# A four-layer sequence model on one core: the first layer's gated experts computed by picked slots in 39 blocks, gate products in column groups, a capacity search in 14 steps

## The reference, cut to what matters

```python
def _L0_ffn_ref(x, gate_w, w_up, w_down, sg_gate, sg_up, sg_down):
    E, TOP_K, HALF = 8, 2, 192
    logits = xf @ gate_w.T
    topk_logits, topk_idx = jax.lax.top_k(logits, TOP_K)
    topk_w = jax.nn.softmax(topk_logits)
    comb = jnp.zeros((N, E)).at[jnp.arange(N)[:, None], topk_idx].add(topk_w)
    for e in range(E):
        y = jax.nn.silu(xf @ wg[e].T) * (xf @ wu[e].T) @ w_down[e].T
        out = out + comb[:, e:e + 1] * y
    shared = jax.nn.silu(xf @ sg_gate.T) * (xf @ sg_up.T) @ sg_down.T
    return shared + out
```

## Time and profile before

| | us |
|---|---|
| median of 3 runs (lowest to highest) | 3692.75 (3686.59 to 3693.5) |
| the profiled execution, its own time | 3684.66 |
| the span of its records | 3683.3 |
| layer 0 routing, 881.03 to 911.05 of the span | 30.0 |
| layer 0 experts, 911.05 to 1267.51 | 356.5 |
| layer 1 search, 2160.94 to 2238.64 | 77.7 |
| layer 1 slots scattered to first block, 2256.28 to 2302.18 | 45.9 |
| layer 1 experts, 2302.18 to 2414.43 | 112.3 |

### The profile page before, as it was taken

One profiled execution on the slowest core, in us unless ns is written; L12 is line 12 of the kernel. 1 busy time (PEld: TensorE's weight loads), 2 busy tenths in 40 slices (PEclk: granted clock), 3 DMA queues, 4 the chain that ended last, 5 costly groups with the idle time before them and its releaser, 6 DMA issues. The chain is left out here.

```text
span 3683.3 us, 43526 instructions
## 1 busy us (share of the span) xinstructions
PE 2919.2 (79%) x12846; PEld 1023.0 (28%) x12846; DVE 2553.5 (69%) x2911; ACT 1819.9 (49%) x3121; POOL 746.6 (20%) x835
## 2 busy tenths in 40 slices
PE   6499999965999948999999551967877787996766
PEld 3122222213333321222222130822322333332222
DVE  4699999934444459989998153267999984446548
ACT  2288888861222226888888310535555541224233
POOL 3311111100000031111110003604777750000000
PEclk8599999986999968999999755987999997998868
DMA  4210110111000040010000220221000000001010
GB/s 121 80 27 24 27 26 23 27 28 62 0 0 0 0 158 22 24 27 23 25 24 18 57 77 30 59 76 37 6 12 6 12 1 0 0 0 56 0 46 23
DMA packets 112034, 116.61 MB, mean 32 GB/s; under 512 B 37102, under 2 KB 88174, under 8 KB 111516
## 3 DMA queue, kind: packets, MB, share of 16 engines
q1 hardware_dynamic: 97116, 83.65, 7.7%
q0 software_dynamic: 14784, 31.43, 2.9%
HBM read 64.25 MB, written 50.75 MB: 31 GB/s over the span
## 5 line engine op out<-in xcount | busy, mean ns | idle before, releaser
L640 DVE TENSOR_REDUCE a_att_mx<-a_att_s 128x2 f32<-128x1024 f32 x1024 | 1204.9, 1218 | 104.4 <-PE a_att_s L551 91.9
L625 ACT ACTIVATE a_att_pt<-a_att_st 128x512 f32<-128x512 f32 x2048 | 1064.6, 604 | 267.8 <-PE a_att_st L577 246.8
L577 PE MATMUL a_att_st<-a_att_qst,a_att_kst 50*128 50x512 bf16 x2048 | 628.8, 389 | 77.8 <-ACT a_att_pt L625 65.0
L551 PE MATMUL a_att_s<-a_att_kst,a_att_qst 50*128 50x512 bf16 x2048 | 532.1, 402 | 84.1 <-DMA a_att_kst<-a_kstk 51.2
L564 PE MATMUL a_att_av<-a_att_pt,a_att_vst 128*32 128x512 f32 x4096 | 554.1, 614 | 0.0
L577 PEld LDWEIGHTS a_att_st<-a_att_qst,a_att_kst 50*128 50x128 bf16 x2048 | 158.9, 94 | 752.2 <-ACT a_att_pt L625 693.7
L929 DVE TENSOR_TENSOR f_h<-f_sg,f_up 128x512 f32<-128x512 f32 x184 | 126.5, 687 | 309.2 <-ACT f_sg L917 309.2
L917 ACT ACTIVATE f_sg<-f_gp 128x512 f32<-128x512 f32 x184 | 109.9, 597 | 460.9 <-PE f_cp L906 460.9
L1701 POOL TENSOR_TENSOR g_xn<-m2s_hs,m2s_cb 128x1024 f32<-128x1024 f32 x128 | 300.9, 2356 | 119.3 <-DVE m2s_hs L1668 66.9
L1668 DVE TENSOR_TENSOR_SCAN m2s_hs<-m2s_da,m2s_bps 128x1024 f32<-128x1024 f32 x128 | 292.7, 2287 | 4.4
L1584 PE MATMUL m2s_yps<-g_xn,g_ident 128*128 128x512 f32 x512 | 242.7, 596 | 0.9
(11 more groups left out here) (396 smaller groups left out, 3502.5 us busy)
## 6 DMA issues: line engine op xcount, KB each, us to landing
a_att_qst<-a_qstk POOLq DMA_DIRECT2D x128, 100.0 KB, 2.5
a_att_kst<-a_kstk POOLq DMA_DIRECT2D x128, 100.0 KB, 2.5
a_qstk<-a_qkv_part SPq DMA_DIRECT2D x96, 128.0 KB, 1.9
a_kstk<-a_qkv_part SPq DMA_DIRECT2D x96, 128.0 KB, 2.0
a_num<-a_att_oev SPq DMA_DIRECT2D x256, 16.0 KB
a_out_nm<-a_num SPq DMA_DIRECT2D x16, 256.0 KB, 3.3
a_out_rb<-a_rden SPq DMA_DIRECT2D x16, 256.0 KB, 4.4
area<-in_f_w_dram SPq DMA_DIRECT2D x2, 2048.0 KB, 10.2
```

The source lines that it names most:

```text
L551: mm = pe.matmul(s1[:, cut % 2, h, :], qst[u][64 * h:64 * h + STACK, qt * P:(qt + 1) * P], kst[u][64 * h:64 * h + STACK, kh * CH:(kh + 1) ...
L577: pe.matmul(st[:, e % 3, :], kst[u][64 * h:64 * h + STACK, kt * P:(kt + 1) * P], qst[u][64 * h:64 * h + STACK, half * CH:(half + 1) * CH], ...
L625: act.activation(pt[:, e % 16, :], st[:, e % 3, :], ACT.Exp, scale=scale).then_inc(exp_done, 1)
L640: dve.tensor_reduce(mx[:, par, 2 * cut:2 * cut + 2], s1[:, cut % 2, :, :], AX.X, ALU.max).then_inc(s1_used, 1)
```

## The change

1. **Layer 0 by slots.** `top2_stage` and `glu_stage` of layer 0 give way to `pick_stage` and `pick_glu_stage`. Each token is written twice, once for each pick, into slots of the pick's expert: 8192 picks in at most 39 blocks of 256 slots, all of which are computed. The shared expert is computed for all tokens on PE while POOL scatters. Each result row is multiplied by its pick's weight and scattered back; at the end PE adds a token's two rows while it turns them (two accumulated products with the identity) and DVE adds them to `g.xT`.
2. **Gate products in column groups** (class `Logits`, layers 0, 1, 2). The gate, padded to 32 columns by POOL, is now the stationary operand and the tokens move: four chunks go to four groups of 32 output rows of the array. ACT copies the rows, PE transposes them (8 of 128 x 128), and DVE picks out the logits.
3. **Capacity search in 14 steps.** Each step tries three thresholds at once (a quarter, a half and three quarters of the interval) and so settles two bits.
4. `gate0` gets one more 64 KB load; the weights of layer 0 are laid out per expert by 13 loads in place of 4, in the same norm stage.

```diff
+class Logits:
+    def pad(self, pool):
+        pool.memset(self.gate32[:, :], 0.0).then_inc(self.padded, 1)
+        pool.wait_ge(self.padded, 1)
+        pool.tensor_copy(self.gate32[:, 0:self.e], self.gate).then_inc(self.padded, 1)
+    def multiply(self, pe, g):
+        pe.wait_ge(self.padded, 2)
+        for m in range(2):
+            for q in range(4):
+                mm = pe.matmul(self.row_ps[32 * q:32 * q + 32, m, :], self.gate32[:, :], g.xn[:, c * CH:(c + 1) * CH], ...)
+            mm.then_inc(self.rows_ready, 1)
...
+def pick_stage(nc, g, name, w, picked):
+                sp.wait_ge(zeroed, 1)
+                sp.dma_start(sent, zero[:, :].unsqueeze(1).to_broadcast([P, n_rows, PICK_WIDE])).then_inc(cleared, 16)
+                sp.wait_ge(cleared, 16)
+                sp.wait_ge(numbered, 1)
+                sp.dma_start(sent[:, :, P:PICK_WIDE], tail[:, :, :]).then_inc(cleared, 16)
+                sp.wait_ge(cleared, 32)
...
+def pick_glu_stage(nc, g, name, w, picked, ahead):
+            def _(pool):
+                for t in range(2 * NT):
+                    pool.indirect_dma_start(picked.sent, ..., rows[:, t, :], None).then_inc(scattered, 16)
+                for i in range(PICK_BLOCKS):
+                    pool.wait_ge(tails_taken, 2 * (i // 3 + 1))
+                    pool.wait_ge(r_copied, wide * (i + 1))
+                    for j in range(wide):
+                        pool.indirect_dma_start(picked.back, ..., yr[:, i % 3, j, :], None).then_inc(r_sent[i % 3], 16)
+            def _(sp):
+                sp.wait_ge(scattered, 16 * 2 * NT)
+                for k in range(groups):
...
+                    sp.dma_start(xs[:, k % 4, :, :], sent[:, 3 * wide * k:3 * wide * (k + 1), :]).then_inc(x_here[k % 4], 16)
...
+                for c in range(NCH // 2):
+                    for r in range(2):
+                        sp.dma_start(got[:, r, 8 * c:8 * c + 8, :], back[:, r, 8 * c:8 * c + 8, :]).then_inc(got_here[c], 16)
+            def _(act):
+                def take_weights(i):
+                    first = act.value_load(expert_i[0:1, i:i + 1], min_val=0, max_val=7) * per_expert
+                    if i >= ring:
+                        act.wait_ge(y_ready, i - ring + 1)
+                    act.copy(wb[:, i % ring, :], own[:, bass.ds(first, per_expert)]).then_inc(w_copied, 1)
...
+                def take_rows(i):
+                    dve.wait_ge(r_turned, i + 1)
+                    dve.wait_ge(tails_taken, 2 * (i // 3 + 1))
+                    if i >= 3:
+                        dve.wait_ge(r_sent[i % 3], 16 * wide * (i // 3))
+                    for j in range(wide):
+                        dve.tensor_scalar(yr[:, i % 3, j, :], rp[:, j * P:(j + 1) * P],
+                                          weight[:, wide * i + j:wide * i + j + 1], None, ALU.mult).then_inc(r_copied, 1)
...
-    e, bits = 8, 28
+    e, bits = 8, 14
...
-                    dve.tensor_tensor(t1[:, :, :], pm[:, :, :], wide_e(cand[:, :]), ALU.is_ge).then_inc(cmp_done, 1)
+                    dve.tensor_tensor(above[:, :, :, :], over_tiles(pm).unsqueeze(1).to_broadcast(four),
+                                      tries[:, :, :].unsqueeze(3).to_broadcast(four), ALU.is_ge).then_inc(cmp_done, 1)
...
-            glu0 = glu_weights("f0", 0, 14, 27)
+            glu0 = pick_weights(nc, g, a, 0)
-                top2_stage(nc, g, "f0r", gate0, combT, 8, False)
-                glu_stage(nc, g, "f0", 14, glu0, combT, 27, (qkv1,))
+                pick_stage(nc, g, "f0r", gate0, picked)
+                pick_glu_stage(nc, g, "f0", glu0, picked, (qkv1,))
```

More of the change, by code:

```diff
@@ new lines, in pick_weights @@
+def pick_weights(nc, g, a, at):
+    made = Weights(nc, g, "f0_pick", [])
+    own = g.area[:, at:at + 8 * 5 * P].rearrange("p (e k q) -> p e k q", e=8, q=P)
+    shared = g.area[:, at + 40 * P:at + 46 * P].rearrange("p (k q) -> p k q", q=P)
+    made.tiles["own"], made.tiles["shared"] = g.area[:, at:at + 40 * P], shared
+    by_expert = lambda n: a[n].rearrange("p t q -> p (t q)")[:, 0:8 * 192].rearrange("p (e r) -> p e r", r=192)
+    gate, up, down = by_expert("f0_wg"), by_expert("f0_wu"), a["f0_wd"]
+    made.moves = [(own[:, :, 0, :], gate[:, :, 0:P]), (own[:, :, 1, :], up[:, :, 0:P]),
+                  (own[:, :, 2, 0:64], gate[:, :, P:192]), (own[:, :, 2, 64:P], up[:, :, P:192]),
+                  (own[:, 0:8:2, 3, :], down[:, 0:12:3, :]), (own[0:64, 0:8:2, 4, :], down[0:64, 1:12:3, :]),
+                  (own[0:64, 1:8:2, 3, :], down[64:P, 1:12:3, :]), (own[64:P, 1:8:2, 3, :], down[0:64, 2:12:3, :]),
+                  (own[0:64, 1:8:2, 4, :], down[64:P, 2:12:3, :]), (own[64:P, :, 4, :], down[64:P, 0:8, :])]
+    made.moves += [(shared[:, 2 * i:2 * i + 2, :], a[n][:, 12:14, :]) for i, n in enumerate(("f0_wg", "f0_wu", "f0_wd"))]
+    made.all, made.end = 16 * len(made.moves), at + 46 * P
+    return made
@@ L975, in top1_stage @@
         over = s.sb("over", [P, e, 16])
[L976 to L979 removed]
+        found = Logits(s, gate, e)
+        cnt_ps, pre_ps, tot_ps = s.ps("cnt", [P, 3 * e]), *(lambda both: (both[:, 0, :], both[:, 1, :]))(s.ps("sums", [P, 2, NT * e]))
+        tps = s.ps("tps", [P, 2, CH])
+        step, turned, copied = (s.sem(x) for x in ("step", "turned", "copied"))
         diff_ready, exp_ready, fin_done = s.sem("diff_ready"), s.sem("exp_ready"), s.sem("fin_done")
@@ L1008, in _ @@
                 pe.wait_ge(w.here, w.all)
-                logits_of(pe, g, ps, gate, e).then_inc(logits, 1)
+                found.multiply(pe, g)
                 pe.matmul(pre_ps[:, 0:1], before_w[:, :], g.ones[:, 0:1], start=True, stop=True).then_inc(place_ps_ready, 1)
-                for t in range(3):
+                for t in range(4):
                     turn(t)
-                for k in range(bits + 1):
-                    turn(k + 3)
+                for k in range(bits):
+                    turn(2 * k + 4)
+                    turn(2 * k + 5)
                     pe.wait_ge(counted_here, k + 1)
-                    pe.matmul(cnt_ps[:, :], g.ones[:, :], part[:, :], start=True, stop=True).then_inc(counted, 1)
+                    pe.matmul(cnt_ps[:, :], g.ones[:, :], parts[:, :, :].rearrange("p j e -> p (j e)"),
+                              start=True, stop=True).then_inc(counted, 1)
+                pe.wait_ge(counted_here, bits + 1)
+                pe.matmul(cnt_ps[:, 0:e], g.ones[:, :], part[:, :], start=True, stop=True).then_inc(counted, 1)
                 pe.wait_ge(eq_ready, 1)
@@ L2100, in build @@
             gate0 = weights("f0", "top2", out0.end, ("gate", [P, 8]), ("desc", [P, 8]))
-            glu0 = glu_weights("f0", 0, 14, 27)
+            gate0.tiles["before"] = g.area[:, gate0.end:gate0.end + P]
+            gate0.moves.append((gate0.tiles["before"], a["f1_before"]))
+            gate0.all += 16
+            glu0 = pick_weights(nc, g, a, 0)
             qkv1 = weights("a1", "qkv", glu0.end, *((k, square) for k in ("wq", "wk", "wv")))
```

420 lines of the change are left out of this document (391 added, 29 removed).

## The result

The changed kernel takes 3545.91 us (median of 4 runs, 3530.75 to 3558.81) against 3689.67 before (4 runs): a ratio of 0.9616, 95% interval 0.9573 to 0.9659. The forecast was 3538 in 3515 to 3580. The profiled execution took 3530.75, and the sum of the prediction for it 3529.7. That is nearer than its steps deserve: layer 0's experts and routing brought 34 and 8 us less than forecast in this trace, and stages that it had left out brought 37 more.

A forecast was written before the change was run, and what follows sets the result against it. PE's matmul columns were taken to bound layer 0's experts, a chain of rounds layer 1's search. Gains -3 + 130.7 + 12.6 + 14.7 = 155.0 took the profiled 3684.66 to 3529.7; 8.1 more for the median gave 3538, range 3515 to 3580.

The forecast's parts named there:

- Part A: Layer 0's routing: 30.0 us before, 33 after, ended by SP's fill and 16-byte writes; range 26 to 47.
- so its pieces took at most 0.85 us, and 9984 take 8.3: Layer 0's routing: 16-byte writes priced at 8.3 us from a bias load's 1024 pieces of 4 bytes.
- Rival (3): Layer 0's routing: the 16-byte pieces go at the rate of whole rows, 14 us more, 3552; chance 0.07.
- Part B: Layer 0's experts: 356.5 us before, 226 after, from scatter, 39 blocks of 2.7 us and the end; gain 130.7.
- That is below 80, so it costs nothing: Layer 0's shared expert, 41 to 50 us and 5 more at low clock, lies hidden under the 80.5 us scatter.
- Rival (6): Layer 0's indirect DMAs: descriptor writing on POOL slows beside DVE; from 2.5 us each slower than before, about 3707; chance 0.02.
- so a 256-column product takes 3.46/8 = 0.43: Layer 0's blocks: five such products and four transposes take PE 2.6 us, priced from layer 1's 3.90 us block.
- rival (2): Layer 0's blocks: handshakes between PE, POOL and DVE lead, 3.3 us a block, 23 us more, 3561; chance 0.20.
- Rival (5): Layer 0's blocks: PE's gaps lose it the clock, 5.3 us a block, 101 us more, 3639; chance 0.06.
- Part C: Gate products in the routing of layers 1 and 2: 6.3 us less each, gain 12.6, within 8 to 15.
- Part D: Layer 1's capacity search: 77.7 us before, 63 after, 14 rounds of 4.5 us; gain 14.7.
- Nothing else.: All other stages were to stay unchanged, 0 us; the 13 weight loads were to cost nothing.

The follow-up runs named there:

- fill_ahead: Changed kernel with the zero fill issued in the first attention's stage instead of layer 0's routing: routing 24.8 us, one run 3523.79 us.
- split_fill: Changed kernel with the 16-byte tails in layer 0's routing written beside the fill, without waiting for it: routing 41.1 us, expert stage 235.6, one run 3513.03 us.
- no_shared: Changed kernel with layer 0's shared expert left out: expert stage 235.7 us, one run 3514.06 us.
- k128: Changed kernel with a block's last down product reading 128 rows, the lower 64 zero, instead of 64: layer 0's expert stage 266.2 us.
- shared_first: Changed kernel with layer 0's first scatter waiting until the shared expert is through: expert stage 286.8 us, one run 3567.75 us.

## Why the prediction was right, and where not

**Part A** (3 more forecast, 10.8 measured). The chain was right: SP ends the stage, DVE is through at 24 us (forecast 26), as fill_ahead showed when it became the bound at 24.8. The fill's 22.2 was 22.7. The step that failed is the price of the pieces, "so its pieces took at most 0.85 us, and 9984 take 8.3": 4-byte reads of a load were no measure for 16-byte writes. They took 15.5 to 16.8 us from issue to landing, 1.5 to 1.7 ns a piece, against the fill's 2.3 ns a row of 528 bytes. Rival (3), at the 22.2 of whole rows, had the direction right and was too dear; the truth lay about in the middle of the two ends. The rule of the Trainium skill, DMA: Bandwidth & Descriptors, section Specifications, that transfers under 512 B are off line rate, held in sign: 156 KB took 16.8 us, 5148 KB 22.7. A piece was not as dear as a whole row, though, as the prediction took the rule to mean.

**Part B** (130.7 less forecast, 97.0 measured). Three terms, and for each the undisturbed kernel split_fill beside it. To the first turned tile: forecast 86.9, 86.3 in split_fill, 103.7 in the changed kernel. From there to the load of the results: forecast 105.3 + 4.4 + 6.7 = 116.4, 125.2 in split_fill, 131.2 in the changed kernel. The end: forecast 22 and 0.5, 24.6 in the changed kernel and 24.2 in split_fill.
"That is below 80, so it costs nothing; it would be the bound only if the scatter took under 55" is the sentence that failed in the first: by length of work it was right (52 us undisturbed, and no_shared was no shorter), but the prediction took two streams on different engines to be independent. In the first trace, and on chips B and C, they were not, and the shared expert took 103 to 109 us. No rival had this. Rival (6) looked for a cost of the indirect DMAs on POOL's side, and there was none: the scatter kept 1.264 to 1.267 us a step in every kernel. The prediction's sign for this step, a shared expert that ends some 25 us before the scatter, was the other way round: it ended 22 us behind it.
In the second term 0.24 us a block, 9.4 in 39, is mis-sized; the other 6.0 between split_fill and the changed kernel are stalls of 0.5 to 2.6 us between some of the blocks, with which PE was busy 91% of the time and not the 95 that the prediction named. The step is "so a 256-column product takes 3.46/8 = 0.43. The new block has five of them": the ruler had products on 128 rows alone, the new block has one on 64, and k128 measured what it costs, 0.35. It was not the handshakes' own lengths: rival (2) at 3.3 us fell, as PE's rhythm of 2.59 in k128 shows. Rival (5) fell too: the granted clock in the blocks was 0.97.

**Part C** (6.3 less each). Layer 2's routing, which has nothing else new, is 8.6 shorter. **Part D** (14.7 less). A round of 4.53 us, forecast 4.5; with part C the stage is 22.7 shorter, forecast 21.0.

**"Nothing else."** This failed by 37 us, 27.1 of them in the attention of layer 1, which the change does not touch. In both traces of before it had six short falls of the granted clock and took 707 us; in the 12 traces with the change, whole or altered, it took 680 to 688 and had none of the six (688 where one fall of 20 us stood at its end, in shared_first and no_shared). That is too regular for chance. What in the change takes them away was not tried: the work ahead of it is other, and so is the time at which it starts. The 20 timed runs of before beside the kernels of chips B and C lay between 3670.8 and 3703.7 us, none at the 3658 that a run without the falls would take by an estimate from the first trace (3684.66 - 27), so most of the 27 us stand in the medians too. The last condition of the prediction, "if a stage of layer 1, 2 or 3 beside these moves", was met, and by it the reasoning is wrong there although the time is right.

**The time.** 154.3 us measured and 155.0 forecast are the sum of errors of -7.8, -33.7, +1.7, +2.3, +27.1 and +9.6, -0.8 in all with rounding. That the total came out so near is chance: without the stall the same steps would have missed it by 24 us.

## What to carry to other kernels

Work that is short enough to lie beneath another engine's stream is hidden only if the signals between its engines arrive; beside back-to-back indirect DMAs, hold a second price ready for every handshake, and measure on more than one chip. Price small DMA pieces by pieces of the same size and direction; when no row has them, carry both ends into the range (here the truth lay in their middle). When a ruler from another stage is laid on a new loop, check each product's rows as well as its columns. And compare every stage after a change, also those that it did not touch: a gain of 15 us in one stage can vanish behind a fall of the clock in another.

## What the runs showed of the hardware

A two-pass product of 256 columns on 64 rows, between products on 128 rows, costs 0.35 us more than one on 128 rows, 2.94 against 2.59 us a block; zeros in the other half cost PE nothing. 9984 pieces of 16 bytes take 15.5 to 16.8 us to land alone, and written beside a full fill they add to it as if behind it (38.6 us in all). Under 64 indirect DMAs issued one behind the other, the completions of TensorE's products reached ACT and DVE in steps of 11.2 and 22.4 us on two chips and at once on a third, in traced runs; the indirect DMAs lost nothing, 1.265 us a step, and SP's wait for their landings ended on time (2.3 us). An attention stage of the same code took 8 to 19 us longer in some executions, with a fall of TensorE's granted clock to half for 20 to 51 us near its end.
